# Merging two of the eight softmax pair sums per quad with an accumulating DMA, and re-slotting the work around them

## The reference, cut to what matters

```python
x = x + tanh(g_xattn) * attention(layernorm(x), ctx, mask, mask, Wq, bq, Wk, bk, Wv, bv)
x = x + tanh(g_ffn)  * ffn(layernorm(x), W2, scale, scale1)

def attention(target, source, tm, sm, ...):            # b = 8, channels 512, t = s = 1024
    q, k, v = Wq @ target + bq, Wk @ source + bk, Wv @ source + bv
    q, k, v = (a.reshape(b, 16, 32, -1) for a in (q, k, v))   # 16 heads of 32 channels
    dot  = einsum('bhdt,bhds->bhts', q, k) / sqrt(32)
    m    = tm[:, :, :, None] * sm[:, :, None, :]
    dot  = m * dot - (1 - m) * 1e6
    amap = softmax(dot, axis=-1) * m
    return einsum('bhts,bhds->bhdt', amap, v).reshape(b, 512, t)

def ffn(x, w, scale, scale1):                          # both factors rounded to fp8 e4m3 first
    return ((x * scale).astype(fp8) / scale) @ ((w * scale1).astype(fp8) / scale1)
```

## Time and profile before

| | |
|---|---|
| median of 3 runs | 2499.71 us (2498.08 to 2499.79) |
| the profiled execution's own time | 2498.55 us |
| its span | 2496.9 us |
| PE busy | 2441.7 us, 98% |
| DVE / ACT / POOL busy | 79% / 56% / 66% |
| one quad in the steady part | 59.6 us |

### The profile page before, as it was taken

One profiled execution on the slowest core, in us unless ns is written; L12 is line 12 of the kernel. 1 busy time (PEld: TensorE's weight loads), 2 busy tenths in 40 slices (PEclk: granted clock), 3 DMA queues, 4 the chain that ended last, 5 costly groups with the idle time before them and its releaser, 6 DMA issues.

```text
span 2496.9 us, 40504 instructions
## 1 busy us (share of the span) xinstructions
PE 2441.7 (98%) x13116; PEld 1382.0 (55%) x13177; DVE 1960.7 (79%) x3259; ACT 1387.1 (56%) x2606; POOL 1643.2 (66%) x1259
## 2 busy tenths in 40 slices
PE   7999999999999999999999999999999999999997
PEld 5888888875444444444444444444444444444442
DVE  6677776687788888888888888888888888888885
ACT  3333333315666666666666666666666666666664
POOL 2443333426777777777777777777777777777775
PEclk9999999999999999999999999999999999999999
DMA  6766666664444444444444444444444444444411
GB/s 245 262 243 237 234 235 235 227 188 100 94 102 98 102 101 102 97 94 95 94 93 100 92 92 92 92 92 101 92 93 95 99 101 102 98 101 97 104 45 56
DMA packets 241807, 313.48 MB, mean 126 GB/s; under 512 B 75000, under 2 KB 142648, under 8 KB 241624
## 3 DMA queue, kind: packets, MB, share of 16 engines
q1 hardware_dynamic: 230776, 275.56, 44.0%
q10 hardware_dynamic: 10848, 35.66, 4.0%
HBM read 199.83 MB, written 101.38 MB: 121 GB/s over the span
## 4 chain that ended last, share of the span: by engine, by line
PE 94%; DVE 1%; DMA 1%; issue 1%; POOL 1%; ACT 1%; SPq 0%; POOLq 0%; ACTq 0%; DVEq 0%
PE bank L863 22%; PE bank L893 20%; PE bank L848 20%; PE bank L878 19%; PE bank L904 9%; PE bank L940 4%; PE bank L933 1%; POOL pair_sum L398 1%; DMA q_st<-qx_scr 0%; DMA w_nat<-in_L_xattn_Wk_dram 0%; DMA v_scr<-stage 0%; ACT probs L715 0%; DVE x_raw L1043 0%; PE bank L802 0%; PE bank L924 0%
## 5 line engine op out<-in xcount | busy, mean ns | idle before, releaser
L398 POOL TENSOR_TENSOR pair_sum<-probs 128x512 f32<-128x512 f32 x1020 | 1279.2, 1286 | 399.0 <-ACT probs L715 399.0
L1143 DVE TENSOR_REDUCE part_max<-bank 128x1 f32<-128x512 f32 x2048 | 1276.6, 682 | 242.7 <-PE bank L878 229.2
L715 ACT ACTIVATE probs<-bank 128x512 f32<-128x512 f32 x2048 | 1067.4, 604 | 601.7 <-PE bank L863 578.7
L863 PE MATMUL bank<-q_st,k_st 100*128 100x512 f32 x2048 | 866.3, 425 | 6.0 <-ACT probs L715 6.0
L878 PE MATMUL bank<-k_st,q_st 98*128 98x512 f32 x2048 | 817.4, 399 | 8.3 <-DVE part_max L1143 6.5
L863 PEld LDWEIGHTS bank<-q_st,k_st 100*128 100x128 f32 x2048 | 387.4, 190 | 410.3 <-issue 211.2
L893 PE MATMUL bank<-probs,v_t 128*32 128x512 f32 x4096 | 545.6, 605 | 0.0
L878 PEld LDWEIGHTS bank<-k_st,q_st 98*128 98x128 f32 x2048 | 388.7, 190 | 129.2 <-DVE part_max L1143 15.8
L389 POOL TENSOR_TENSOR stage_lo<-stage,stage_hi 128x512 fp32r<-128x512 f32 x128 | 186.6, 1483 | 137.7 <-ACT stage_hi L661 136.2
L904 PE MATMUL bank<-pair_sum,ones 128*32 128x512 f32 x2040 | 265.5, 592 | 0.0
L661 ACT ACTIVATE stage_hi<-stage 128x512 fp32r<-128x512 f32 x128 | 80.2, 633 | 205.1 <-DVE stage L1007 142.9
(11 more groups left out here) (112 smaller groups left out, 2007.3 us busy)
## 6 DMA issues: line engine op xcount, KB each, us to landing
k_st<-k_scr SPq DMA_DIRECT2D x96, 512.0 KB
q_st<-q_scr SPq DMA_DIRECT2D x192, 256.0 KB
c_raw<-in_ctx_dram ACTq DMA_DIRECT2D x32, 512.0 KB, 7.0
k_scr<-stage_hi SPq DMA_DIRECT2D x64, 256.0 KB, 2.5
k_scr<-stage_lo SPq DMA_DIRECT2D x64, 256.0 KB, 2.7
v_scr<-stage SPq DMA_DIRECT2D x64, 256.0 KB, 2.9
q_scr<-stage_hi SPq DMA_DIRECT2D x64, 256.0 KB, 2.4
q_scr<-stage_lo SPq DMA_DIRECT2D x64, 256.0 KB, 2.7
```

The lines of the kernel that those rows point to most:

```text
L398: nc.gpsimd.tensor_tensor(pair_sum[:, r % 2, h], probs[:, a, h], probs[:, a + 1, h], ALU.add).then_inc(pair_done, 1)
L715: nc.scalar.activation(probs[:, c % PR, h, :], s_bank_of(n, k)[:, :], ACT.Exp).then_inc(exp_done, 1)
L863: nc.tensor.matmul(s_bank_of(n, k)[:, :], k_st[p][0:KS, h, j * P:(j + 1) * P], q_st[p][0:KS, th, h, :], start=True, stop=True).then_inc(sc ...
L1143: nc.vector.tensor_reduce(part_max[:, th, sh, at:at + 1], x_bank_of(n, "tile", k)[:, :], AX, ALU.max).then_inc(max_done, 2)
```

## The change

What it does, part by part:

1. Four sum buffers in place of two: the two halves of `pair_sum`, and `stage` and `stage_hi`, which the first part has done with. POOL waits before the third sum of the first quad (n = 0, r = 2) until all stores from `stage` have landed.
2. After pair sums 1 and 5 POOL issues a DMA that adds buffer 0 to buffer 1 (128x2048 float32, 1 MB, SBUF to SBUF, `merge`). PE then has six groups of denominators a quad in place of eight: the sums r = 2, the merged 0+1, 3 of the first half at slots 27, 35, 43; r = 6, the merged 4+5, 7 of the second at 59 and, in the next period, 3 and 11.
3. The FFN matmuls move from slots 31 and 47 to 39 and 51; the last rounding steps on DVE from slot 19 to 27.
4. The maxima are split by reductions, with the negation on ACT (`minus_high`, slots 20 and 52) and the low part at slots 22 and 54 (`low_max`); the negation's sign moves to the identity.
5. `invert` keeps only the reciprocal (slots 19 and 51). ACT multiplies mask by gate once a quad (`mask_gates`, slot 46), and POOL applies the product (`mask_inverse`) after pair sum 2 and after pair sum 6 (in the last quad after 5).
6. `weigh` is split by halves (after pair sums 2 and 3). The power stands between the first and second addition of pair sum 5.
7. SP's queue: the queries of the two halves are stacked apart, the first half of quad n+2 in the middle of period n; the last stores of the first part stand ahead of the second half of the queries of quad 1; `set_max` goes ahead of `move_inv`, `turn_y8` behind `spread_inv`.
8. In the last quad the pair sums 6 and 7 are not formed: PE sums their chunks directly (16 records in place of 8 each); before, only 7 was done so.

The diff, cut to its core:

```diff
-            STACK_DMAS = (8, 4)
+            STACK_DMAS = 4
-            F_JOBS = {23: "max1", 31: "ffn0", 47: "ffn1", 55: "max0"}
+            F_JOBS = {23: "max1", 39: "ffn0", 51: "ffn1", 55: "max0"}
+            DEN_AT = {27: 0, 35: 1, 43: 2, 59: 3}
+            DEN_AFTER = {3: 4, 11: 5}
+            NG = 6
+            SUM_OF_GROUP = (2, 1, 3, 6, 5, 7)
+            sums = [pair_sum[:, 0], pair_sum[:, 1], stage[:, :, :], stage_hi[:, :, :].bitcast(F32)]
...
                     def add_pair(n, r):
-                        if counted(SJ * n + r - 1):
-                            pool.wait_ge(den_done, SJ * n + r - 1)
+                        wait_sum_free(n, r)
                         for h in range(QH):
+                            if (r, h) == (5, 1) and n > 0:
+                                invert_std_2(n - 1)
                             pool.wait_ge(exp_done, NSLOT * n + 2 * QH * r + QH + h + 1)
-                            nc.gpsimd.tensor_tensor(pair_sum[:, r % 2, h], probs[:, a, h], probs[:, a + 1, h],
+                            nc.gpsimd.tensor_tensor(sums[r % 4][:, h], probs[:, a, h], probs[:, a + 1, h],
+                    def merge(n, th):
+                        pool.wait_ge(pair_done, QH * (SJ * n + 4 * th + 2))
+                        pool.dma_start(sums[1], sums[0], accum_op=ALU.add).then_inc(merged[th], 16)
+                    def mask_inverse(m, th):
+                        pool.wait_ge(inv_done, 2 * (2 * m + th) + 1)
+                        pool.wait_ge(gates_masked, m + 1)
+                        nc.gpsimd.tensor_tensor(inv_c[:, :], inv_c[:, :], gtm_c[:, th], ALU.mult).then_inc(inv_done, 1)
                     def period(n, p):
                         for r in range(SJ):
-                            if real(n) and (n, r) != (LAST, SJ - 1):
+                            if n == 0 and r == 2:
+                                wait_stage_free()
+                            if real(n) and (n < LAST or r < SJ - 2):
                                 add_pair(n, r)
+                            if real(n) and r % 4 == 1:
+                                merge(n, r // 4)
+                            if r == 2 and ordinary(n - 1):
+                                mask_inverse(n - 1, 1)
+                                weigh(n - 1, 0)
+                            if r == (5 if n == LAST else 6) and real(n):
+                                mask_inverse(n, 0)
                             if r == 3 and ordinary(n - 1):
-                                weigh(n - 1)
+                                weigh(n - 1, 1)
                                 add_residual(n - 1, 1 - p)
...
-                    def denominators(m, r):
-                        th, i = r // 4, r % 4
+                    def denominators(m, g):
+                        th, i = g // 3, g % 3
+                        r = SUM_OF_GROUP[g]
-                        pe.wait_ge(pair_done, QH * SJ * m + QH * (r + 1))
+                        if i == 1:
+                            pe.wait_ge(merged[th], 16 * (m + 1))
+                        else:
+                            pe.wait_ge(pair_done, QH * SJ * m + QH * (r + 1))
...
-                        if k == 23 and ordinary(n - 1):
-                            invert(n - 1, 1)
-                        if k == 55 and real(n):
-                            invert(n, 0)
+                        if k == 22 and real(n):
+                            low_max(n, 1)
+                        if k == 54 and real(n + 1):
+                            low_max(n + 1, 0)
+                        if k == 19 and ordinary(n - 1):
+                            invert(n - 1, 1)
+                        if k == 51 and real(n):
+                            invert(n, 0)
```

More of the change, by code:

```diff
@@ L176, in flamingo_gated_layer @@
         init_done = sem("init_done")
-        stacked = [sem(f"stacked{i}") for i in range(TH)]
+        k_stacked = sem("k_stacked")
+        q_stacked = [sem(f"q_stacked{i}") for i in range(TH)]
         v_loaded = [sem(f"v_loaded{i}") for i in range(2)]
@@ L187, in flamingo_gated_layer @@
         pair_done = sem("pair_done")
+        merged = [sem(f"merged{i}") for i in range(TH)]
         pv_done = sem("pv_done")
@@ L588, in period @@
                             load_v(n + 1, 1 - p)
+                        if real(n) and real(n + 2):
+                            stack_q(n + 2, 0, p)
                         if real(n):
@@ L785, in _ @@
                     act.wait_ge(ident_done, 2)
-                    nc.scalar.activation(ident_r[:, :], ident_f[:, :], ACT.Copy).then_inc(ident_copied, 1)
+                    nc.scalar.activation(neg_ident[:, :], ident_f[:, :], ACT.Copy, scale=-1.0).then_inc(ident_copied, 1)
                     split_ctx(0)
@@ L1265, in period @@
                         for k in range(NSLOT):
[L1266 removed]
+                            if n - 1 == LAST and k == 28:
                                 finish_last(LAST, 1 - p)
```

220 lines of the change are left out of this document (137 added, 83 removed).

## The result

The change made the kernel slower. Four executions of the changed kernel took 2522.16 us in the median (2516.58 to 2532.22); beside them the kernel before took 2499.75 (2498.08 to 2500.7). The ratio is 1.0091, with a 95% interval of 1.0073 to 1.011. The forecast was 2468. The profiled execution took 2516.58 us with a span of 2514.8, 17.9 over the span before.

What follows compares the result with a forecast made beforehand. PE, busy 98%, was taken as the bound. A quad: -1.74 + 0.60 + 0.20 = -0.94 us; times 31 -29.1, last quad and tail -1.9, together -31: forecast 2468 us, 8-in-10 range 2442 to 2491.

Steps and rivals of the forecast that it cites:

- What is removed: On PE, two denominator groups of eight a quad go, at 0.87 us each: 1.74 us a quad less.
- (1) The sum at slot 27: PE waits 0.30 us for POOL's pair sum 2 at slot 27, and again for sum 6 at 59: +0.60 a quad.
- (2) Issuing the merge: On POOL between pair sums 1 and 2, a 1.3 us issue overruns a 1.11 us hole: +0.20 us a quad.
- Rival B: Issuing the merge costs POOL 2.4 us and overruns both holes: +0.42 us a quad, 2510 us; chance 8%.
- (3) The merge's landing: The 1 MB lands in 10.3 us (bounds 4.1 and 21.1), before PE needs it at 12 us: cost nothing.
- Rival C: The merge lands late, at 15 us in place of 12: +4 us a quad, 2620 us; chance 6%.
- The maxima: On DVE before turn_max, about 2.7 us of work fits a 2.87 us gap: cost 0, other end 0.6 a quad.
- The rest of a quad at nothing: mask_inverse, weigh in halves, and SP's spread and y8 cost 0; PE sees nothing of a slip under 2 us.
- Rival D: Several thin covers (turns 0.6, POOL's slack) take up the gain: -0.34 us a quad, 2486 us; chance 10%.
- Ends: Start 0 (bounds 2 us either way); last quad -0.87 and 1 us for the tail without POOL's additions: together -1.9.
- the theory T: Experiments' theory: merge traffic delays the inverse's small store, SP's queue passes it to the keys, whose end meets later loads.

Runs made afterwards that it cites:

- e6: The changed kernel without its two merges a quad; PE adds both pair sums of each itself (64 denominator records a quad, as before): 2527.4 us, ratio 1.0103.
- e1: The changed kernel with each merge cut to 4 of the 512 columns of every head, still issued and waited for: 2489.13 us, ratio 0.9953.
- e8: e7 with turn_y8 issued ahead of spread_inv and the last quad's second merge left to PE: 2475.43 us, ratio 0.99.
- e10: The changed kernel with only the last quad's second merge left to PE: 2508.59 us, ratio 1.0033.
- e5: The kernel before with 2 x 1 MB of accumulating DMA a quad added between two unused buffers, in quads 1 to 31: 2554.5 us, ratio 1.0233.
- e9: e6 with the first half's inverse stored twice, the second time only when the first has landed: 2547.74 us, ratio 1.0173.
- e2: The changed kernel with the key load (stack_k) ahead of spread_inv in SP's queue: 2484.72 us, ratio 0.993.
- e3: The changed kernel with the keys' four-row transfer (kx) made only in two of every four quads: 2492.45 us, ratio 0.9961.
- e12: The changed kernel with residual rows cut to 8 of 128 and second-half query parts to 2 of 32 rows, from the third block: 2485.95 us, ratio 0.9936.
- e7: e2 with the edit of e3 added: 2484.68 us, ratio 0.9931.
- e11: e8 without the kx edit, so the keys' four extra rows are loaded in every quad: 2474.72 us, ratio 0.989.

## Why the prediction was wrong

By its own steps:

- **What is removed**, 1.74 a quad: right, e6 and the good quads show 1.71.
- **(1) The sum at slot 27**, +0.60: right in place and near in size. The wait is 0.25 at slot 27. At slot 59 a wait shows in 8 quads alone, but the tiles behind it start 0.34 later all the same (e6), and all that the change adds beside the merges is 0.72.
- **(2) Issuing the merge**, +0.20: the rule was right, the size too large. The issue is 0.88 us behind 0.30 of waiting for the sum, 1.18 against a hole of 1.11: nothing. At 1.31, in e1, the quads are 0.43 longer, exactly 1.31 - 0.88 and once a quad, as the two holes were worked out. Rival B had the right mechanism and fails by its price of 2.4.
- **(3) The merge's landing**, 10.3 us with a cover of 12: 6.9 to 13.2, and no wait for it. Rival C fails. The estimate of 8 us from the Trainium skill ("DMA: Bandwidth & Descriptors", "Bandwidth") lies near the 8.6 measured.
- Their sum, 58.7 us a quad, is what the good quads take, to 0.03.
- **The maxima**, 0: right.
- **"The rest of a quad at nothing"**: here it failed. The step looked at SP only for the spread ahead of `weigh` and for y8, both in the first half of a quad. It did not list what stands behind the other spread, that of slot 55: the 1.5 MB of keys, which PE needs at slot 19. It counted `mask_inverse` as POOL's time alone, "where POOL has a hole", while behind sum 6 it holds the store back from +0.88 to +3.46. And "PE sees nothing of a slip under 2 us" is refuted: slips of 1.1 to 1.5 us came with 3.2 to 7.4 more in a quad. In step (3) I priced the 1 MB by its own landing alone, "cost nothing", and never asked whose transfers it would slow. Rival D, thin covers, went by the right suspicion and priced turns and POOL, not the queue. The loss is 40.6 us in the quads, against the 1.5 that the good ones gained over the forecast.
- **Ends**: the start is 2.9 us longer in this execution, but e6 and e8, with the same first part, begin at 559.0 and 559.1 (before: 558.4; others up to 562.9). Most of it is a difference between executions. The tail's -1.9 became +5.1, and e10 gives back 3.5 of it by taking one merge away: the last merge sits 1.6 us ahead of the last inverse. POOL's four slow additions are gone as forecast, and DVE's rounding (L90 to L101) takes 5.1 us in place of 9.0. DVE did not gain by it, since it then sits idle for the spread inverse, 9.35 us, and 3.75 in e10, where its last reciprocal still comes 1.5 later than before. Here the forecast also misread: in the kernel before DVE was busy without a pause from 2462.57 to 2474.50, so that its reciprocal hung on DVE's own work, and that PE's last group ended 0.07 us earlier was chance.

Against a forecast of -31, 39 us are the quads', 7 the tail's and 3 the start's: the 49 between -31 and +18.

The Trainium skill has the sentence that speaks against the step: the page "DMA: Bandwidth & Descriptors", section "Issuing engines are not separate DMA queues", says that transfers ordered by GpSimd run on the same 16 engines as SP's and interleave with them. The trace agrees where a merge is in flight: in e5 the store is ordered in the middle of one, lands only behind it and takes 2.2 to 4.3 us instead of 1.4 (from the fourth quad on); in the tail of the changed kernel it takes 7.7. Its section "Latency and other measured facts" adds that access to HBM takes ten times as long at high load, which would lengthen just such a store; no run here tells that from the queueing.

In the quads, though, the theory T had its first link wrong: the merge does not run beside the store of the first half. In five of the 11 quads with a long store it had landed 0.2 us behind the store's issue, and the store still took 3.2 or 3.3. Merges alone bring the other 19 to 1.9 us in the median. What the long ones have in common, with merges or without (e1, e6, e9), is the packet of q8. Without merges it meets the first half's store in three quads (e6), with them in 11.

What is shown, and what isn't. The bytes of the merges make more stores long (e1, e5, e6). The order of the queue carries a long store to the keys (e2). At the orders of the changed kernel it is the four-row transfer that then comes too late (e3). A late order is enough without any merge (e9), the loads at +20 amplify it (e12), and the tail's 3.5 us are the last merge (e10). That the long stores are those with a packet of q8 in them is read from traces (the changed kernel, e1, e2, e6, e9; e3, e7 and e12 have an exception or two), and that the merges delay this packet and so bring it into the store is a reading of e1 beside the changed kernel; no run moved the packet by itself. Not settled is why the ordinary quads of e5 are 1.1 us longer than before, of which the waits name only a part, and why in e10 keys ordered at +6.35 came late twice.

## What to carry to other kernels

A transfer has two prices: when it lands, and what it does to the transfers around it. For each new one list the small transfers that come beside it or right behind it, and for each of these what stands behind it in its queue, down to the large load that somebody needs at a fixed slot. The queues that the kernel did not order, here `instruction`, belong on the list. And a small step moved to another engine moves all that waits for it: ask what `mask_inverse` holds back, not what it costs. An in-order queue should order the large load with a deadline ahead of anything that waits for a round trip through HBM. Where PE is at 98%, count a wait on it at more than its length: 2.8 us of idling came with 1.7 of lower clock.

The kernel that this leads to beats both: e11 at 0.989 and e8 at 0.99 of the time before, 2475 us. The merges are its gain, and two calls moved in SP's queue the condition for it.

## What the runs showed of the hardware that I had not expected

- An accumulating DMA of 1 MB from SBUF to SBUF costs POOL 0.88 us to issue; with 128 times fewer bytes in rows of 4 elements it costs more, 1.31 (e1). The page counts 33792 packets on q0 for those merges and 9216 for the whole ones: here the price followed the packets and not the bytes.
- A store of 8 KB, 1.4 us in the median without merges (e6), takes 2.2 to 4.3 when it is ordered in the middle of a transfer of 1 MB (first half, e5), and 7.7 in the tail of the changed kernel. Right behind a merge it takes 1.9 in the median, and 3.2 to 3.7 when one 16 KB packet of the `instruction` queue starts within it.
- A transfer into four rows can be the late one while three wide ones ordered just ahead of it land in time: with it, orders at +7.4 to +7.8 cost 3.2 to 7.4 us in eight quads; without it, at +7.3 to +7.6, nothing in eight (e3).
- A load's lateness is magnified by what its end meets: the order of the keys came 0.2 us later than one that was free (+7.2) and the quad took some 4 us more (+7.4), though one at +7.7 took 58.84. With the later loads cut away the long ones took 1.3 to 2.9 more (e12).
